# Transposing two MLP pieces at once, and placing the first piece's first product inside the attention's tail

## The chip, the cores and the metric

The kernel runs on one core of a Trainium2 chip. The metric is device time in microseconds for one execution. The kernel before took 525.93 us (median of 3 runs, 525.63 to 526.66). All durations below come from one profiled execution, which took 525.39 us and whose span, from its first to its last instruction, is 523.4 us.

## What is computed

The input x has 32 images of 32 by 32 positions with 64 channels, in float32. The reference is one block of a windowed transformer:

```
h = layernorm(x); roll by (-4,-4); cut into 8x8 windows
q,k,v = h @ qkv_w + qkv_b          # 4 heads of 16
attn = softmax(q k^T / 4 + relative position bias + mask)
x = x + roll_back(attn @ v @ proj_w + proj_b)
h2 = layernorm(x)
out = x + gelu(h2 @ fc1_w + fc1_b) @ fc2_w + fc2_b     # 64 -> 256 -> 64
```

## The kernel before

x stays in SBUF for the whole kernel, 128 partitions by 8 groups (GROUPS) of four images' rows. The attention runs first, as 64 steps (PAIRS) plus a tail of 4 (TAIL). Which tasks run at which step is a fixed list (TASKS, lines 81 to 98): XT transposes, QK and V products, Y the output projection. The last two Y tasks, (Y, last group, 0) and (Y, last group, 1), come at step 67.5, after everything else of the attention.

Then comes the MLP with its layer norm, in 32 pieces (S); a piece is 128 partitions by 512 numbers. Each engine has its own program and executes it in that order; semaphores are the only link. For a piece p the work is:

- DVE `sum2` (row sums, L406), GpSimd `centre2` (mean L323, then subtraction L338), ScalarE `square` (L590), DVE `square_sum` (L412), GpSimd `rstd` (add eps L330, then power -0.5, L333), DVE `scale_rows` (L420). That is the layer norm, and it leaves the piece in `xn`, which holds four pieces.
- TensorE `transpose_piece` (L829) into one of two PSUM banks, ScalarE `copy_xT2` (L672) into the buffer `xT2`.
- TensorE `fc1`, two halves of 4 instructions each (trans and outs, L693), ScalarE `gelu` per half (L678), TensorE `fc2` (work, 64 instructions, L693).
- DVE adds the result to x (L570, called out below) and has before that added the last bias to x (L581, called bf2 add below). SP stores.

The orders in the MLP, written out by hand, s counting from 0:

- TensorE (L887): transposes of s+1, fc1(s), fc2(s-1).
- ScalarE (L683): copy s+1, gelu(s) twice, square(s+3).
- DVE (L565): out(s-2), sum2(s+4), scale_rows(s+2), square_sum(s+3), bf2 add(s).
- GpSimd (L397): centre2(s+4) with its mean first, then rstd(s+3).

`centre2(s+4)` waits for the sum of that piece (L322) and for the transposes of piece s, whose place in `xn` it takes (L351). `scale_rows(u)` waits for rstd(u) (L417). `square(s+3)` stands behind both gelus of s on ScalarE. `fc1(s)` waits for the copy of s and for the gelus of s-1; `fc2(s)` for gelu(s) and for out(s-2). Transposes wait for the scaled piece.

Of the kernel before, what the change touches and what calls it, by code (L numbers as in the profile page):

```python
# [8 lines left out]
ACT = mybir.ActivationFunctionType  # L9
# [3 lines left out]
P = 128  # L13
BATCH, SIDE, C = 32, 32, 64
# [5 lines left out]
GROUPS = BATCH // GI  # L20
ROW = SIDE * C
PIECE = WIN * C
PIECES = ROW // PIECE
STEPS = 2 * GI
PAIRS = STEPS * GROUPS
BANK = 512
IMG = 4 * P
S = GROUPS * PIECES
# [37 lines left out]
TR, PV, OUT = 1, 2, 3  # L66
# [30 lines left out]
def tasks_at(n):  # L97
    return [task[1:] for task in TASKS if task[0] == n]
# [28 lines left out]
def build(nc, x_d, params_d, out_d):  # L127
    with ExitStack() as ctx:
        def sb(name, *shape, dtype=F32):
            return ctx.enter_context(nc.sbuf_tensor(name, [P, *shape], dtype))  # L130
# [57 lines left out]
        w1 = sb("w1", FF)  # L188
        bqkv = sb("bqkv", 2)
        bf1 = sb("bf1", 2)  # L190
        xT2 = [sb(f"xT2_{i}", BANK) for i in range(2)]
        hidden = [[probs[2 * i + half] for half in range(2)] for i in range(2)]


        xT2_bank = [scores[:, 0:BANK], scores[:, BANK:2 * BANK]]
        fc1_bank = [trans, outs2]
# [6 lines left out]
        w1_ready, biases_summed = sem("w1_ready"), sem("biases_summed")  # L203
        scores_ready, scores_taken = sem("scores_ready"), sem("scores_taken")
        negmax_ready, shifted, probs_ready = sem("negmax_ready"), sem("shifted"), sem("probs_ready")
        trans_ready, trans_copied = sem("trans_ready"), sem("trans_copied")
        outs_ready, inverse_ready, outs_taken = sem("outs_ready"), sem("inverse_ready"), sem("outs_taken")
        oT_ready, oT_copied = sem("oT_ready"), sem("oT_copied")
# [10 lines left out]
        xT2_ready, xT2_copied = sem("xT2_ready"), sem("xT2_copied")  # L219
        fc1_ready, gelu_done = sem("fc1_ready"), sem("gelu_done")  # L220
# [183 lines left out]
        def _(dve):  # L404
# [11 lines left out]
            def scale_rows(u, j):  # L416
                dve.wait_ge(ln_rstd, u + 1)  # L417
                chunk = xn[:, j * PIECE:(j + 1) * PIECE].rearrange("q (a f) -> q a f", f=C)
                r = stat_rstd[:, j * WIN:(j + 1) * WIN].unsqueeze(2).to_broadcast([P, WIN, C])
                nc.vector.tensor_tensor(chunk, chunk, r, ALU.mult).then_inc(xn_ready, 1)  # L420

            for t in range(2):
                done = nc.vector.memset(vX[t][:, :, :], 0.0)
# [4 lines left out]
            for column in ones:  # L428
                done = nc.vector.memset(column, 1.0)
# [6 lines left out]
            for half, i in ((second_half, 1), (first_half, 2), (second_half, 2), (first_half, 3),  # L436
                            (second_half, 3)):
                dst, src, c0, n = half(0, i)
# [124 lines left out]
            dve.wait_ge(y_added, COUNT["Y", GROUPS - 1, 1])  # L563

            for s in range(S + 2):  # L565
                if s >= 2:
                    dve.wait_ge(y2_ready, s - 1)
                    dve.wait_ge(bf2_added, s - 1)
                    dst = x[:, (s - 2) * PIECE:(s - 1) * PIECE]
                    nc.vector.tensor_tensor(dst, work[s % 2], dst, ALU.add).then_inc(out_ready, 1)  # L570
                if s + 4 < S:
                    sum2(s + 4)
                if PIECES <= s + 2 < S:
                    scale_rows(S + s + 2, (s + 2) % PIECES)
                if PIECES <= s + 3 < S:
                    square_sum(S + s + 3, (s + 3) % PIECES)
                if s < S:

                    dve.wait_ge(ln_centred, S + s + 1)
                    dst = x[:, s * PIECE:(s + 1) * PIECE].rearrange("q (a f) -> q a f", f=C)  # L580
                    nc.vector.tensor_tensor(dst, dst, bf2[:, :].unsqueeze(1).to_broadcast([P, WIN, C]),  # L581
                                            ALU.add).then_inc(bf2_added, 1)

        @block.scalar
        def _(act):
# [60 lines left out]
            def copy_oT(n):  # L646
# [6 lines left out]
                    outsT[:, 0:2 * P].rearrange("q (i a r) -> q i a r", i=2, r=WIN), ACT.Copy)\  # L653
                  .then_inc(oT_copied, 1)

            for n in range(PAIRS + TAIL):
                if n < PAIRS:
                    exp(n)
                squares_of(n)
                for kind, of, i in tasks_at(n):  # L660
                    take(kind, of, i)
                if 0 <= n - TR < PAIRS:
                    copy_trans(n - TR)
                if 0 <= n - OUT < PAIRS:
                    copy_oT(n - OUT)
                for kind, of, i in tasks_at(n + 0.5):
                    if kind != "Y":
                        take(kind, of, i)

            def copy_xT2(s):  # L670
                act.wait_ge(xT2_ready, s + 1)
                nc.scalar.activation(xT2[s % 2][:, :], xT2_bank[s % 2], ACT.Copy)\  # L672
                  .then_inc(xT2_copied, 1)

            def gelu(s):
                for half in range(2):
                    act.wait_ge(fc1_ready, 2 * s + half + 1)
                    nc.scalar.activation(hidden[s % 2][half][:, :], fc1_bank[half][:, :],  # L678
                                         ACT.Gelu_apprx_tanh, bias=bf1[:, half:half + 1])\
                      .then_inc(gelu_done, 1)  # L680

            copy_xT2(0)
            for s in range(S):  # L683
                if s + 1 < S:
                    copy_xT2(s + 1)
                gelu(s)
                if PIECES <= s + 3 < S:
                    square(S + s + 3, (s + 3) % PIECES, S + s + 4)

        @block.tensor  # L690
        def _(pe):
            def mm(out, lhsT, rhs, start=True, stop=True):
                return nc.tensor.matmul(out, lhsT, rhs, start=start, stop=stop)  # L693
# [127 lines left out]
            def transpose_piece(s):  # L821
                pe.wait_ge(xn_ready, S + s + 1)
                if s >= 2:
                    pe.wait_ge(xT2_copied, s - 1)
                else:
                    pe.wait_ge(scores_taken, PAIRS)
                for k in range(4):
                    at = s % PIECES * PIECE + k * P
                    done = nc.tensor.transpose(xT2_bank[s % 2][:, k * P:(k + 1) * P],  # L829
                                               xn[:, at:at + P], ident[:, :])  # L830
                done.then_inc(xT2_ready, 1)

            for kind, of, i in tasks_at(-1):
                if kind == "XT":
                    warm(2)
                fill(kind, of, i)
                if (kind, i) == ("QK", 0):
                    score(0)
            for n in range(PAIRS + TAIL):
                if n + 1 < PAIRS:  # L840
                    score(n + 1)
                for kind, of, i in tasks_at(n):
                    fill(kind, of, i)
                if 0 <= n - PV < PAIRS:
                    weigh(n - PV)
                if 0 <= n - TR < PAIRS:
                    transpose_probs(n - TR)
                if 0 <= n - OUT < PAIRS:
                    transpose_o(n - OUT)
                for kind, of, i in tasks_at(n + 0.5):  # L850
                    fill(kind, of, i)
                if n in (PAIRS, PAIRS + 1):
                    transpose_piece(n - PAIRS)

            pe.wait_ge(w1_ready, 1)
            pe.wait_ge(trans_copied, PAIRS)
            pe.wait_ge(oT_copied, PAIRS)
            copied("Y", GROUPS - 1, 1)

            def fc1(s):  # L860
                pe.wait_ge(xT2_copied, s + 1)
                for half in range(2):
                    if s:
                        pe.wait_ge(gelu_done, 2 * s - 1 + half)
                    for w in range(2):
                        rows = slice(C * w, C * (w + 1))
                        done = mm(fc1_bank[half][:, w * BANK:(w + 1) * BANK],
                                  w1[rows, half * P:(half + 1) * P], xT2[s % 2][rows, :])
                    done.then_inc(fc1_ready, 1)

            def fc2(s):

                if s >= 2:
                    pe.wait_ge(out_ready, s - 1)
                pe.wait_ge(gelu_done, 2 * s + 2)
                for k in range(4):
                    for w in range(2):
                        to = (2 * k + w) * C
                        for half in range(2):
                            for part in range(2):  # L880
                                at = w * BANK + k * P + part * C
                                done = mm(work[s % 2][C * part:C * (part + 1), to:to + C],
                                          hidden[s % 2][half][:, at:at + C], w2[:, half, :],
                                          start=half == 0, stop=half == 1)
                done.then_inc(y2_ready, 1)

            for s in range(S + 1):  # L887
                if 2 <= s + 1 < S:
                    transpose_piece(s + 1)
                if s < S:  # L890
                    fc1(s)
                if s:
                    fc2(s - 1)


def pack_params(ln1_g, ln1_b, qkv_w, qkv_b, proj_w, proj_b, rpb, ln2_g, ln2_b, fc1_w, fc1_b, fc2_w,
# [37 lines left out]
```

## Time and profile before

| | |
|---|---|
| median of 3 runs | 525.93 us |
| the profiled execution | 525.39 us |
| its span | 523.4 us |
| attention with its tail | 0 to 371 us |
| MLP, first fc1 to last add | 371 to 518 us |
| last stores | to 523.4 us |
| TensorE (PE) busy | 464.8 us |
| DVE / ScalarE / GpSimd busy | 391.3 / 361.6 / 384.0 us |
| granted TensorE clock, mean | 0.984 |

Busy is the time in which an engine had an instruction under way. PEld is TensorE's loading of weights, which overlaps its products. A row of the timeline has the start, the busy time, the engine, the line, what it writes and reads, and in square brackets how long the engine had been idle before it and what ended this.

### The profile page before, as it was taken

To read this page: it belongs to the slowest core of one execution; us is meant where nothing else is said; L and a number is where in the kernel's file an instruction comes from. 1 tells how busy PE (TensorE), PEld (TensorE's weight loads), DVE (VectorE), ACT (ScalarE), POOL (GpSimd) and SP (SyncE) were. 2 spreads that over 40 slices of the span, in tenths; PEclk is the share of its full clock that TensorE was granted. 3 is DMA by queue.
4 is the path that set the end of the run, shared out by engine and by line. 5 is a ranking of instruction groups with operands and counts; after the bars stand their busy time and mean duration, and the time that the engine had idled before them with its cause. 6 is when DMAs were issued, how large, how long until landed. Compare 5 with 4: busy or idle time off the path is not lost.

```text
span 523.4 us, 21507 instructions
## 1 busy us (share of the span) xinstructions
PE 464.8 (89%) x9630; PEld 351.7 (67%) x9630; DVE 391.3 (75%) x549; ACT 361.6 (69%) x501; POOL 384.0 (73%) x376
## 2 busy tenths in 40 slices
PE   0766798999999899899899899998799999999995
PEld 0534676777787787777778678687466666666664
DVE  2766797988889888888888888894367766666752
ACT  0245679768877867868878868775477777777762
POOL 2658889869868869869868968941278888888830
PEclk9997999999999999999999999999799999999998
DMA  8201441411501500511111011000003203311333
GB/s 160 58 1 41 105 94 42 113 24 28 118 23 25 123 23 24 117 29 24 27 30 33 23 29 38 23 23 3 1 3 84 66 19 81 83 39 46 82 83 81
DMA packets 9986, 27.04 MB, mean 52 GB/s; under 512 B 3368, under 2 KB 3368, under 8 KB 7976
## 3 DMA queue, kind: packets, MB, share of 16 engines
q1 hardware_dynamic: 9896, 25.68, 21.0%
q8 instruction: 76, 1.25, 1.0%
q14 instruction: 14, 0.11, 0.1%
HBM read 9.15 MB, written 8.39 MB: 34 GB/s over the span
## 4 chain that ended last, share of the span: by engine, by line
PE 61%; POOL 11%; DVE 11%; ACT 11%; issue 3%; DMA 2%; SPq 0%; ACTq 0%; DVEq 0%
PE work L693 20%; PE outs L693 13%; PE trans L693 8%; PE trans L789 7%; POOL probs L367 6%; PE scores L693 5%; PE scores L829 4%; ACT vX L612 3%; PE work L708 3%; ACT probsT L643 3%; DVE negmax L482 3%; POOL stat_rstd L333 3%; DVE probs L476 2%; DMA params<-in_params 2%; POOL xn L344 2%
## 5 line engine op out<-in xcount | busy, mean ns | idle before, releaser
L367 POOL TENSOR_TENSOR probs<-probs,negmax 128x1024 f32<-128x1024 f32 x64 | 121.7, 1902 | 36.0 <-DVE negmax L482 36.0
L333 POOL TENSOR_TENSOR stat_rstd<-stat_var,minus_half 128x8 f32<-128x8 f32 (+1 forms) x62 | 104.9, 1692 | 5.0
L476 DVE TENSOR_TENSOR probs<-scores,bias 128x1024 f32<-128x1024 f32 x64 | 77.9, 1218 | 28.4 <-PE scores L693 28.4
L638 ACT ACTIVATE probs<-probs 128x1024 f32<-128x1024 f32 x64 | 67.7, 1058 | 33.1 <-POOL probs L367 32.6
L643 ACT ACTIVATE probsT<-trans 128x1024 f32<-128x1024 f32 x64 | 65.6, 1024 | 31.8 <-PE trans L789 31.4
L693 PEld LDWEIGHTS outs<-vX,probsT 128*64 128x64 f32 x2048 | 65.0, 138 | 31.8 <-issue 29.4
L338 POOL TENSOR_TENSOR xn<-x,stat_mean 128x256 f32<-128x256 f32 (+1 forms) x91 | 77.2, 866 | 4.1
L482 DVE TENSOR_REDUCE negmax<-probs 128x16 f32<-128x1024 f32 x64 | 78.1, 1220 | 2.2
L693 PEld LDWEIGHTS work<-params,probs 128*64 128x64 f32 x2048 | 62.2, 138 | 23.5 <-DVE x L570 20.5
L693 PE MATMUL scores<-kX,qT 32*64 32x128 f32 x2048 | 71.5, 276 | 7.2 <-DVE probs L476 4.6
L693 PE MATMUL outs<-vX,probsT 128*64 128x34 f32 x2048 | 72.1, 225 | 2.2 <-ACT probsT L643 1.4
L789 PE MATMUL trans<-ident,probs 128*128 128x128 f32 x512 | 70.8, 282 | 0.0
L693 PE MATMUL work<-params,probs 128*64 128x64 f32 x2048 | 66.5, 223 | 0.0
L693 PEld LDWEIGHTS scores<-kX,qT 32*64 32x64 f32 x2048 | 55.9, 133 | 15.1 <-DMA kX<-kT 6.6
L412 DVE TENSOR_REDUCE stat_sq<-squares 128x8 f32<-128x512 f32 x64 | 43.0, 680 | 29.5 <-ACT squares L590 29.4
L789 PEld LDWEIGHTS trans<-ident,probs 128*128 128x128 f32 x512 | 55.5, 142 | 4.3 <-issue 1.6
L678 ACT ACTIVATE probs<-trans,bf 128x1024 f32<-128x1024 f32 x32 | 35.7, 1115 | 21.9 <-PE trans L693 21.9
L323 POOL TENSOR_TENSOR stat_mean<-stat_sum,one_over_c 128x8 f32<-128x8 f32 (+2 forms) x54 | 18.0, 334 | 43.6 <-DVE stat_sum L406 42.3
L590 ACT ACTIVATE squares<-xn 128x512 f32<-128x512 f32 x64 | 39.1, 621 | 15.3 <-DVE xn L439 15.3
L406 DVE TENSOR_REDUCE stat_sum<-x 128x8 f32<-128x512 f32 x64 | 42.2, 677 | 8.4 <-DMA x<-in_x 8.3
L330 POOL TENSOR_TENSOR stat_var<-stat_sq,eps 128x8 f32<-128x8 f32 (+1 forms) x62 | 23.3, 375 | 31.9 <-DVE stat_sq L412 31.9
L693 PE MATMUL work<-xT,wqkv 64*64 64x512 f32 x256 | 36.6, 629 | 7.8 <-DVE x L533 2.7
(64 smaller groups left out, 698.8 us busy)
## 6 DMA issues: line engine op xcount, KB each, us to landing
kX<-kT SPq DMA_DIRECT2D x124, 64.0 KB, 2.0
x<-in_x SPq DMA_DIRECT2D x32, 224.0 KB
out<-x SPq DMA_DIRECT2D x28, 224.0 KB
x<-in_x SPq DMA_DIRECT2D x32, 32.0 KB
out<-x SPq DMA_DIRECT2D x28, 32.0 KB
out<-x SPq DMA_DIRECT2D x16, 56.0 KB
params<-in_params SPq DMA_DIRECT2D x1, 741.5 KB, 11.8
out<-x SPq DMA_DIRECT2D x16, 8.0 KB
```

Source lines behind the costliest of these rows:

```text
L333: nc.gpsimd.tensor_tensor(stat_rstd[:, cols], stat_var[:, cols], minus_half[:, cols], ALU.pow).then_inc(ln_rstd, pieces)
L338: return nc.gpsimd.tensor_tensor(dst, src.rearrange("q (a f) -> q a f", f=C), m, ALU.add)
L367: nc.gpsimd.tensor_tensor(e, e, top, ALU.add).then_inc(shifted, 1)
L406: nc.vector.tensor_reduce(stat_sum[:, r * WIN:(r + 1) * WIN], src.rearrange("q (a f) -> q a f", f=C), AXX, ALU.add, negate=True).then_inc( ...
L412: nc.vector.tensor_reduce(stat_sq[:, r * WIN:(r + 1) * WIN], squares[r % PIECES][:, :].rearrange("q (a f) -> q a f", f=C), AXX, ALU.add).t ...
L476: nc.vector.tensor_tensor(e[:, :].rearrange("q (u a m) -> q a u m", u=2, a=2), scores[:, :].rearrange("q (a u m) -> q a u m", a=2, u=2), b ...
L482: nc.vector.tensor_reduce(negmax[n % 4][:, :], e[:, :].rearrange("q (a m) -> q a m", m=N), AXX, ALU.max, negate=True).then_inc(negmax_read ...
L590: nc.scalar.activation(squares[j % PIECES][:, :], xn[:, j * PIECE:(j + 1) * PIECE], ACT.Square, scale=float(C) ** -0.5).then_inc(ln_square ...
L638: nc.scalar.activation(probs[n % 4][:, :], probs[n % 4][:, :], ACT.Exp)\
L643: nc.scalar.activation(probsT[n % 2][:, :], trans[:, :], ACT.Copy)\
L693: return nc.tensor.matmul(out, lhsT, rhs, start=start, stop=stop)
L789: done = nc.tensor.transpose(trans[:, t * P:(t + 1) * P], probs[n % 4][:, t * P:(t + 1) * P], ident[:, :])
```

## The change

The transposes of the pieces s+1 and s+2 now stand together, for odd s, between fc1(s) and fc2(s-1); before, those of s+1 stood ahead of fc1(s). `xT2` has four buffers and not two. ScalarE copies both pieces behind gelu(s) for odd s; square(s+3) follows the copies. On DVE, scale_rows(s+2) moves from behind out(s-2) and sum2(s+4) to ahead of both. fc1(0) leaves the MLP: its first half is put in step 66 of the attention's loop, its second half between the two last Y tasks; ScalarE copies pieces 0 and 1 inside that loop too. GpSimd's program is not touched.

```diff
-        xT2 = [sb(f"xT2_{i}", BANK) for i in range(2)]
+        xT2 = [sb(f"xT2_{i}", BANK) for i in range(4)]
...
             for s in range(S + 2):
+                if PIECES <= s + 2 < S:
+                    scale_rows(S + s + 2, (s + 2) % PIECES)
                 if s >= 2:
                     dve.wait_ge(y2_ready, s - 1)
                     dve.wait_ge(bf2_added, s - 1)
@@
                 if s + 4 < S:
                     sum2(s + 4)
-                if PIECES <= s + 2 < S:
-                    scale_rows(S + s + 2, (s + 2) % PIECES)
                 if PIECES <= s + 3 < S:
                     square_sum(S + s + 3, (s + 3) % PIECES)
...
+                if n in (PAIRS, PAIRS + 1):
+                    copy_xT2(n - PAIRS)
...
-            copy_xT2(0)
             for s in range(S):
-                if s + 1 < S:
-                    copy_xT2(s + 1)
                 gelu(s)
+                if s % 2:
+
+                    for t in (s + 1, s + 2):
+                        if t < S:
+                            copy_xT2(t)
                 if PIECES <= s + 3 < S:
                     square(S + s + 3, (s + 3) % PIECES, S + s + 4)
...
                 for kind, of, i in tasks_at(n + 0.5):
                     fill(kind, of, i)
+                    if (kind, of, i) == ("Y", GROUPS - 1, 0):
+                        fc1(0, 1)
                 if n in (PAIRS, PAIRS + 1):
                     transpose_piece(n - PAIRS)
-
-            pe.wait_ge(w1_ready, 1)
-            pe.wait_ge(trans_copied, PAIRS)
-            pe.wait_ge(oT_copied, PAIRS)
+                if n == PAIRS + OUT - 1:
+
+                    pe.wait_ge(w1_ready, 1)
+                    pe.wait_ge(trans_copied, PAIRS)
+                    fc1(0, 0)
+
             copied("Y", GROUPS - 1, 1)
...
-            for s in range(S + 1):
-                if 2 <= s + 1 < S:
-                    transpose_piece(s + 1)
+            for s in range(1, S + 1):
                 if s < S:
-                    fc1(s)
-                if s:
-                    fc2(s - 1)
+                    for half in range(2):
+                        fc1(s, half)
+                if s % 2:
+                    for t in (s + 1, s + 2):
+                        if t < S:
+                            transpose_piece(t)
+                fc2(s - 1)
```

## Rows read from the trace of the kernel before

**Rows 1.** Busy time by engine, a stretch of the MLP: PE, PEld, DVE, ACT, POOL.
```profile
420.00:440.00 20.00, 20.00 (x350) 13.90 (x346) 13.88 (x23) 14.06 (x19) 16.44 (x18) 1.00 0.23 56
```
**Rows 2.** Chain that ended last, same stage: start, us, work.
```profile
387.47 2.02 PE work L693 x64
```
**Rows 3.** Timeline of one piece in the MLP's steady state, all engines.
```profile
385.42 0.68 DVE L581 TENSOR_TENSOR x<-x,params 128x512 f32<-128x512 f32 x1
...
385.48 1.13 PE L693 MATMUL trans<-xT,w 64*128 64x512 f32 x4
385.58 0.58 POOL L330 TENSOR_TENSOR stat_var<-stat_sq,eps 128x8 f32<-128x8 f32 x1 [0.58 <-DVE stat_sq L412]
...
386.01 0.68 DVE L570 TENSOR_TENSOR x<-work,x 128x512 f32<-128x512 f32 x1
...
386.24 1.65 POOL L333 TENSOR_TENSOR stat_rstd<-stat_var,minus_half 128x8 f32<-128x8 f32 x1
386.45 1.02 PE L693 MATMUL outs<-xT,w 64*128 64x512 f32 x4
...
386.62 0.68 DVE L406 TENSOR_REDUCE stat_sum<-x 128x8 f32<-128x512 f32 x1
...
387.40 2.08 PE L693 MATMUL work<-params,probs 128*64 128x64 f32 x64
...
387.85 0.20 POOL L323 TENSOR_TENSOR stat_mean<-stat_sum,one_over_c 128x8 f32<-128x8 f32 x1
387.92 0.69 DVE L420 TENSOR_TENSOR xn<-xn,stat_rstd 128x512 f32<-128x512 f32 x1 [0.63 <-POOL stat_rstd L333]
388.13 1.38 POOL L338 TENSOR_TENSOR xn<-x,stat_mean 128x512 f32<-128x512 f32 x1
388.67 0.63 ACT L590 ACTIVATE squares<-xn 128x512 f32<-128x512 f32 x1
389.33 0.69 DVE L412 TENSOR_REDUCE stat_sq<-squares 128x8 f32<-128x512 f32 x1 [0.72 <-ACT squares L590]
...
389.42 0.66 PE L829 MATMUL scores<-ident,xn 128*128 128x128 f32 x4
...
390.00 1.13 PE L693 MATMUL trans<-xT,w 64*128 64x512 f32 x4
390.10 0.58 POOL L330 TENSOR_TENSOR stat_var<-stat_sq,eps 128x8 f32<-128x8 f32 x1 [0.58 <-DVE stat_sq L412]
```
**Rows 4.** Timeline of TensorE in an attention step: eight transposes.
```profile
349.16 1.09 PE L789 MATMUL trans<-ident,probs 128*128 128x128 f32 x8
```
**Rows 5.** Instructions of single lines: ns min/median/max; the third is GpSimd's subtraction.
```profile
L517 DVE TENSOR_TENSOR x<-x,y_bias x16: 1215/1783/2966, 54.4 to 348.4; 128x1024 f32<-128x1024 f32 x16
...
L330 POOL TENSOR_TENSOR stat_var<-stat_sq,eps x62: 200/208/585, 19.4 to 503.1; 128x8 f32<-128x8 f32 x60, 128x16 f32<-128x16 f32 x2
...
L338 POOL TENSOR_TENSOR xn<-x,stat_mean x28: 1042/1378/1380, 372.3 to 496.6; 128x512 f32<-128x512 f32 x28
```
**Rows 6.** Timeline of the attention's tail and the MLP's first product.
```profile
365.49 1.08 ACT L672 ACTIVATE xT<-scores 128x512 f32<-128x512 f32 x2
365.74 1.16 PE L693 MATMUL work<-params,oT 64*64 64x64 f32 x64 [0.56 <-ACT oT L651]
...
368.23 1.16 PE L693 MATMUL work<-params,oT 64*64 64x64 f32 x64 [1.34 <-DVE x L527]
...
371.07 2.08 PE L693 MATMUL trans<-xT,w 64*128 64x512 f32 x4 [1.68 <-DVE x L533]
```
**Rows 7.** Busy time by engine and granted clock (last but two) around that product.
```profile
366.80:370.27 3.47, 1.26 (x71) 1.02 (x64) 2.03 (x3) 1.07 (x1) 0.00 (x0) 1.00 0.02 5
370.27:377.10 6.83, 6.03 (x16) 2.75 (x18) 2.43 (x5) 2.76 (x3) 2.83 (x4) 0.50 0.00 0
```
**Rows 8.** Timeline of the MLP's end: last first product, last add.
```profile
511.46 1.13 PE L693 MATMUL trans<-xT,w 64*128 64x512 f32 x4
...
517.37 0.69 DVE L570 TENSOR_TENSOR x<-work,x 128x512 f32<-128x512 f32 x1 [1.18 <-PE work L693]
```

More of the change, by code:

```diff
@@ L654, in copy_oT, with copy_xT2 @@
                   .then_inc(oT_copied, 1)
+            def copy_xT2(s):
+                act.wait_ge(xT2_ready, s + 1)
+                nc.scalar.activation(xT2[s % 4][:, :], xT2_bank[s % 2], ACT.Copy)\
+                  .then_inc(xT2_copied, 1)
             for n in range(PAIRS + TAIL):
@@ L668, in _ @@
                         take(kind, of, i)
[L670 to L673, printed above, removed]
+                if n in (PAIRS, PAIRS + 1):
+                    copy_xT2(n - PAIRS)
             def gelu(s):
@@ L831, in transpose_piece, with fc1 @@
                 done.then_inc(xT2_ready, 1)
+            def fc1(s, half):
+                pe.wait_ge(xT2_copied, s + 1)
+                if s:
+                    pe.wait_ge(gelu_done, 2 * s - 1 + half)
+                for w in range(2):
+                    rows = slice(C * w, C * (w + 1))
+                    done = mm(fc1_bank[half][:, w * BANK:(w + 1) * BANK],
+                              w1[rows, half * P:(half + 1) * P], xT2[s % 4][rows, :])
+                done.then_inc(fc1_ready, 1)
             for kind, of, i in tasks_at(-1):
@@ L851, in _ @@
                     fill(kind, of, i)
+                    if (kind, of, i) == ("Y", GROUPS - 1, 0):
+                        fc1(0, 1)
                 if n in (PAIRS, PAIRS + 1):
                     transpose_piece(n - PAIRS)
-            pe.wait_ge(w1_ready, 1)
-            pe.wait_ge(trans_copied, PAIRS)
-            pe.wait_ge(oT_copied, PAIRS)
+                if n == PAIRS + OUT - 1:
+                    pe.wait_ge(w1_ready, 1)
+                    pe.wait_ge(trans_copied, PAIRS)
+                    fc1(0, 0)
             copied("Y", GROUPS - 1, 1)
-            def fc1(s):
-                pe.wait_ge(xT2_copied, s + 1)
-                for half in range(2):
-                    if s:
[L864 to L869, printed above, removed]
             def fc2(s):
@@ L885, in fc2 @@
                 done.then_inc(y2_ready, 1)
-            for s in range(S + 1):
-                if 2 <= s + 1 < S:
-                    transpose_piece(s + 1)
+            for s in range(1, S + 1):
                 if s < S:
-                    fc1(s)
-                if s:
-                    fc2(s - 1)
+                    for half in range(2):
[5 more added lines that the diff above has]
+                fc2(s - 1)
 def pack_params(ln1_g, ln1_b, qkv_w, qkv_b, proj_w, proj_b, rpb, ln2_g, ln2_b, fc1_w, fc1_b, fc2_w,
```

## The prediction

> **What bounds the kernel now.** I read the busy time by stretch first, to see which engine is full in the stage that changes, then the chain of waits, then the timeline of one piece. In the MLP's steady state TensorE is busy for all of 20.00 us, GpSimd for 16.44, ScalarE and DVE for about 14 [rows 1]. The chain there is TensorE alone; its costliest link is the second product with 2.02 us [rows 2]. The timeline gives the steps of TensorE, start to start: first half of fc1 0.97 (385.48 to 386.45), second half 0.95 (to 387.40), fc2 2.02 (to 389.42), four transposes 0.58 (to 390.00). The sum is 4.52 us a piece [rows 3]. Nothing of this is a wait. The layer norm runs beside it with little to spare: GpSimd waited 0.58 us for the sums of squares and DVE 0.63 us for rstd, once a piece [rows 3]. So the question is not only what TensorE saves, but whether the norm's ring through DVE and GpSimd still closes within a piece's time. It has to be followed in the order of the programs.
>
> **What TensorE saves.** Eight transposes took 1.09 us [rows 4] and four took 0.66 [rows 3], so four more in the same run cost 0.43 and not 0.58. A pair of pieces would take 0.97+0.95+0.58+0.43+2.02+0.97+0.95+2.02 = 8.89 us against 9.04. The switches from fc1 to transposes and from transposes to fc2 are not in the trace; the nearest are fc1 to fc2 (in the 0.95) and transposes to fc1 (in the 0.58). I give them 0.1 either way, so 15 pairs save 2.3 us, between -0.7 and 5.3, if nothing waits.
>
> fc1(0) leaves the path. Its first half now stands where TensorE was idle for 0.56 us [rows 6] and takes 0.97, so the first of the two last projections starts 0.4 later at most; I take 0.4. Its second half (0.95) lies in the 1.34 us in which TensorE waits for DVE between them [rows 6], and costs nothing; were that idle time not there, it would cost its 0.95. The copies of pieces 0 and 1 on ScalarE (1.08 for both) started at 365.49 [rows 6] and now stand ahead of the last copy of the attention's output by one copy; it is inside the same 0.4. fc1(1) can then start at 371.07 + 0.4 = 371.47, where fc1(0) started. Two more buffers of xT2 cost no time.
>
> **What the move on DVE does.** This decides. GpSimd's order stays centre2(s+4), rstd(s+3). Before, DVE issued sum2(s+4) ahead of scale_rows(s+2), so that GpSimd got its sum while DVE waited for rstd. Now DVE waits for rstd(s+2) first, and out(s-2), sum2(s+4), square_sum(s+3) and the bf2 add are queued behind that wait. rstd(s+3) on GpSimd stands behind centre2(s+4), which needs sum2(s+4). This closes a ring with one piece in it: scale(k), out, sum2(k+2), mean, centre2(k+2), rstd(k+1), scale(k+1). A faster TensorE does not shorten it. Its length, call the start of scale(k) zero:
>
> - scale to out 0.61 and out to sum2 0.61 (one DVE step each, 386.01 to 386.62) [rows 3];
> - sum2 to mean 0.77 (as 389.33 to 390.10, DVE's reduction to GpSimd's next), mean to subtraction 0.28 (387.85 to 388.13) [rows 3]: the subtraction starts at 2.27 and takes 1.04, its shortest time [rows 5], to 3.31;
> - DVE reaches the bf2 add at 0.61 x 4 = 2.44, while GpSimd subtracts. An addition of two SBUF operands on DVE does not run beside a GpSimd one: that of L517 took between 1215 and 2966 ns for the same work [rows 5], and the subtraction took 1378 instead of 1042 where a scale_rows had started just ahead of it [rows 3, 5]. So I let the add wait until 3.31. From the start of such an add to the start of the power is 0.82 (385.42 to 386.24), which is 4.13;
> - power to scale_rows 1.68 (386.24 to 387.92) [rows 3]. The ring takes 5.81 us.
>
> Without the add in the way the step from add-eps to power would be 0.28 (as mean to subtraction; add-eps itself takes 200 ns at least) and the ring 0.61+0.61+0.77+0.28+1.04+0.28+1.68 = 5.27. If the mean too were held up (585 instead of 200 ns) and the subtraction took 1.38, it would be 6.53 [rows 5]. I take 5.81, for which each meeting has its row.
>
> The Trainium skill (SBUF — State Buffer, SBUF: two separate sides) says that GpSimd and a DVE instruction with two SBUF inputs take a shared pair of ports as an exclusive lock, for a whole instruction. The trace agrees with its 1215 to 2966 ns. By that rule the ring is 5.81, without it 5.27, which is 14 us over the kernel.
>
> TensorE needs 8.89/2 = 4.45 a piece, so it waits for the ring. Is anything slower than the ring? The squares of an odd piece t stand behind both gelus of t-3 and meet an earlier deadline than before: from fc1(t-3) to square(t) 3.19 (385.48 to 388.67), to its sum 0.66, to add-eps 0.77, to the power 0.66 (385.58 to 386.24), to scale_rows 1.68, and 0.77 to its transposes (0.69 and an estimated hand-over of 0.08): 7.73 us [rows 3]. fc1(t-3) starts 0.58 + 2.02 after the transposes of t-2; together 10.33 us a pair, less than the ring's 2 x 5.81 = 11.62. So the ring ends last, and TensorE stands idle once a pair for 11.62 - 8.89 = 2.7 us, between the transposes of an even and of an odd piece.
>
> **The sum.** fc1(1) at 371.47. square(4) follows it by 3.19 and the two copies, 1.08 [rows 6], at 375.74; its sum 0.66, add-eps 0.77, power 0.66 and 1.68 later scale(4) starts, at 379.51. The ring goes round for each k from 4 to 29: 26 x 5.81 = 151.1, scale(30) at 530.6. Piece 31 has no subtraction before it: 0.61+0.61+0.77+0.66+1.68 = 4.33, scale(31) at 534.9, its transposes at 535.7. Then, with nothing in the way, transposes 0.58, fc2 2.02, fc1 1.92, fc2 2.02, and from the last fc1 to the last add 5.91 (511.46 to 517.37) [rows 8]: 548.1. From the last add to the end of the span were 6.03 us, the span to the time 1.99, and the profiled execution lies 0.54 below the median: 556.7 us. To this I add 2 for the clock (below): 558.5 us, 33 slower than 525.93.
>
> **The clock.** In the MLP's first 6.83 us TensorE had 1.2 GHz granted, after a stretch of 3.47 us in which it was busy for 1.26 [rows 7]; four instructions took 2.08 us there against 1.13 [rows 3, 6]. With fc1(0)'s second half in that stretch it is busy for 2.2, and the fall may stay out. But the new gaps of 2.7 us are of the same kind. A fall costs little while the ring has slack: the squares' path above, held against the ring, has 1.3 us a pair. Over 6.83 us at that ratio 6.83 - 6.83 x 1.13/2.08 = 3.1 us of work are lost, so up to 1.8 in such a pair. I count one such fall in the forecast.
>
> **The rivals.**
>
> A. TensorE's order alone decides (faster). It needs the ring under 4.45 us, that is that DVE's sums run ahead of the scaling after all. For it: the 0.58 and 0.63 of slack [rows 3], and TensorE the bound everywhere. Against it: the two waits stand in the programs. From fc1(1) at 371.47, 15 x 8.89 to fc1(31) at 504.8, 5.9 to the last add at 510.7 instead of 517.4: 519.3 us.
>
> B. The ring is looser than I read it, and only the squares' path holds: 14 odd pieces (5 to 31) at 10.33 - 8.89 = 1.44 each on A's time, 539.5 us. For it: the steps of GpSimd could be shorter when it does not wait. Against it: the ring would have to be under 5.2, below its shortest rows.
>
> C. TensorE's clock falls in every gap. The squares' path then ends last in each pair: 13 x 1.8 on 556.7 is 580 us. For it: the row of 1.26 in 3.47 us [rows 7]. Against it: TensorE works for 8.9 us without a break between gaps. The Trainium skill (TensorE: Matmul & The Clock Gate, HAM oscillation — how this bites in real kernels) tells of a kernel that lost its clock in every wait for a transfer. That speaks against this change; here the trace shows one fall in front of the MLP and none inside it, where TensorE never waited.
>
> **How the numbers follow.** Forecast 0.80, A 0.05, B 0.06, C 0.07; 0.02 is left for a result within 0.2% of before, which is about what a measurement can tell from no change (gain and loss in balance by accident). The range: the short ring (5.27) gives 542.7 + 2 for the clock, about 545; upward a ring of 6.2 gives 567, with two or three falls of the clock 571. B and C lie outside. Faster is A, 0.05; slower 0.93.
>
> **What would show it.** In the profile after: the scale_rows instructions about 5.8 us apart all through, with DVE waiting some 1.8 us ahead of each for the power, and GpSimd waiting ahead of each mean for the row sum, about 2 us (before: not at all); TensorE idle once a pair for 2.7 us ahead of the transposes, released by DVE; the chain led by GpSimd and DVE instead of TensorE. The saving on TensorE is right if a pair without the gap is 8.9 us. fc1(0)'s halves should stand ahead of and between the last two projections, and fc1(1) start near 371.5. The prediction is wrong if sum2 is seen to start before the power of two pieces earlier has ended, or if the distance between scalings is under 5.2 us.

## The result, and the profile after

The changed kernel took 557.27 us (median of 4 runs, 555.46 to 558.25) against 525.78 us before on the same chip: 1.0594 times as long, 95% interval 1.0559 to 1.0629. Forecast were 558.5 us, within 545 to 571. The profiled execution took 558.25 us with a span of 556.2 us, 32.8 more than before.

The chain that ended last, from the page of the changed kernel, led by TensorE with 61% before, now runs over four engines. Over the whole kernel TensorE still has the largest share; between 385 and 535 us, where the loss arises, GpSimd leads it with 22.0% for the power, 9.7% for the subtraction and 8.0% for add-eps, against 12.9% for TensorE's fc2.

```profile
PE 38%; POOL 25%; ACT 13%; DVE 12%; issue 9%; DMA 2%; SPq 0%; POOLq 0%; ACTq 0%; DVEq 0%
```

The stretch that [rows 1] shows before, in the same columns. TensorE was busy for all of it; now it is for 16.55 us of 20, at a mean granted clock of 0.91, and no other engine is full either. So no engine's amount of work sets the pace here. The next two views show what does.

```profile
420.00:440.00 20.00, 16.55 (x258) 11.44 (x260) 12.05 (x18) 10.78 (x15) 11.46 (x13) 0.91 0.22 54
```

The view of who waited for whom, between 390 and 530 us (total us, times, longest). Each of DVE and GpSimd now waits for the other once a piece, 24 times each, by amounts that do not vary (48.0 us in 24 waits is 2.0 each, which is also the longest); TensorE waits for the scaling once a pair.

```profile
POOL stat_mean L323 <- DVE stat_sum L406: 48.0, 24, 2.0
...
DVE xn L420 <- POOL stat_rstd L333: 43.8, 24, 1.8
...
PE scores L833 <- DVE xn L420: 21.7, 12, 2.3
```

One turn of the ring and the start of the next, from the timeline of the changed kernel, to be held against [rows 3]. It is read down: addition, row sum, mean, subtraction, add-eps, power, scaling, addition.

```profile
427.34 0.68 DVE L572 TENSOR_TENSOR x<-work,x 128x512 f32<-128x512 f32 x1
...
427.94 0.68 DVE L406 TENSOR_REDUCE stat_sum<-x 128x8 f32<-128x512 f32 x1
...
428.70 0.20 POOL L323 TENSOR_TENSOR stat_mean<-stat_sum,one_over_c 128x8 f32<-128x8 f32 x1 [2.00 <-DVE stat_sum L406]
...
428.98 1.04 POOL L338 TENSOR_TENSOR xn<-x,stat_mean 128x512 f32<-128x512 f32 x1
429.13 1.44 DVE L581 TENSOR_TENSOR x<-x,params 128x512 f32<-128x512 f32 x1
...
429.98 0.66 POOL L330 TENSOR_TENSOR stat_var<-stat_sq,eps 128x8 f32<-128x8 f32 x1
430.23 0.42 PEld L833 LDWEIGHTS scores<-ident,xn 128*128 128x128 f32 x4 [0.76 <-issue]
430.24 0.65 PE L833 MATMUL scores<-ident,xn 128*128 128x128 f32 x4
...
430.71 1.65 POOL L333 TENSOR_TENSOR stat_rstd<-stat_var,minus_half 128x8 f32<-128x8 f32 x1
...
432.39 0.69 DVE L420 TENSOR_TENSOR xn<-xn,stat_rstd 128x512 f32<-128x512 f32 x1 [1.83 <-POOL stat_rstd L333]
433.00 0.68 DVE L572 TENSOR_TENSOR x<-work,x 128x512 f32<-128x512 f32 x1
...
433.14 0.66 PE L833 MATMUL scores<-ident,xn 128*128 128x128 f32 x4 [2.25 <-DVE xn L420]
```

From addition to addition 5.66 us (427.34 to 433.00). The bf2 add took 1.44 us instead of 0.68: it waited for the subtraction to end at 430.02, and add-eps behind it took 0.66 instead of 0.20. TensorE's even piece was transposed at 430.24, the odd one had to wait until 433.14.

The next turn took 5.70 us (scaling to scaling, 432.39 to 438.09), and its last wait is another. Here add-eps starts 0.76 us behind the start of the sum of squares, the usual hand-over. That sum had waited for its square, and the square stood on ScalarE behind the copy of the odd piece:

```profile
433.83 0.60 ACT L658 ACTIVATE xT<-scores 128x512 f32<-128x512 f32 x1 [1.73 <-PE scores L833]
434.32 0.62 ACT L590 ACTIVATE squares<-xn 128x512 f32<-128x512 f32 x1
...
434.98 0.69 DVE L412 TENSOR_REDUCE stat_sq<-squares 128x8 f32<-128x512 f32 x1 [0.70 <-ACT squares L590]
...
435.74 0.58 POOL L330 TENSOR_TENSOR stat_var<-stat_sq,eps 128x8 f32<-128x8 f32 x1
```

So a second ring of nearly the same length lies beside the first: scaling, transposes, copy, square, sum of squares, add-eps, power, scaling. Turns of 5.66 and of 5.69 to 5.73 alternate, but for those behind a fall of TensorE's clock (below).

**Where the 32.8 us of the span are.** scale(4) started at 380.36 (before 383.40): -3.0. From there to scale(30) 150.1 us passed against 117.5: +32.6. From scale(30) to scale(31) 6.16 against 4.51: +1.6. From scale(31) to the last add 13.19 against 11.94: +1.2. The last stores: +0.4.

### The profile page after: what moved, and what is told of

Its sections match the earlier page's. It is cut to its first block, busy times and chain, and to the rows that moved or that the text cites. A ratio compares the mean times of both kernels' runs of the same rounds, so it can differ in the third digit from the quotient of the medians.

```text
span 556.2 us, 21537 instructions
## 1 busy us (share of the span) xinstructions
PE 471.5 (85%) x9630; PEld 358.1 (64%) x9630; DVE 394.3 (71%) x549; ACT 359.9 (65%) x501; POOL 376.7 (68%) x376
## 4 chain that ended last, share of the span: by engine, by line
PE 38%; POOL 25%; ACT 13%; DVE 12%; issue 9%; DMA 2%; SPq 0%; POOLq 0%; ACTq 0%; DVEq 0%
PE work L697 12%; POOL stat_rstd L333 10%; PE outs L697 8%; PE trans L793 7%; POOL probs L367 7%; PE scores L697 3%; ACT vX L612 3%; PE work L712 3%; ACT probsT L643 3%; POOL xn L338 3%; POOL stat_var L330 3%; PE trans L697 3%; ACT probs L680 2%; POOL xn L344 2%; DVE stat_sq L412 2%
## 5 line engine op out<-in xcount | busy, mean ns | idle before, releaser
L697 PEld LDWEIGHTS work<-params,probs 128*64 128x64 f32 x2048 | 69.3, 150 | 14.8 <-issue 12.6
L697 PE MATMUL work<-params,probs 128*64 128x64 f32 x2048 | 73.7, 236 | 0.0
L338 POOL TENSOR_TENSOR xn<-x,stat_mean 128x256 f32<-128x256 f32 (+1 forms) x91 | 68.5, 772 | 4.1
L420 DVE TENSOR_TENSOR xn<-xn,stat_rstd 128x512 f32<-128x512 f32 x32 | 22.0, 691 | 52.6 <-POOL stat_rstd L333 52.6
```

What stands on the lines that cost most here:

```text
L338: return nc.gpsimd.tensor_tensor(dst, src.rearrange("q (a f) -> q a f", f=C), m, ALU.add)
```

## The experiments

In all of them the ratio is to the kernel before, run beside it on the same chip; the experiments ran on three chips, so kernels are best compared by ratio. The single runs of the kernel before lay between 522.14 and 528.66 us over the three sets.

**The move on DVE alone.**

```
             for s in range(S + 2):
+                if PIECES <= s + 2 < S:
+                    scale_rows(S + s + 2, (s + 2) % PIECES)
                 if s >= 2:
...
-                if PIECES <= s + 2 < S:
-                    scale_rows(S + s + 2, (s + 2) % PIECES)
```

> The kernel before with one edit: on DVE scale_rows(s+2) stands ahead of out(s-2) and sum2(s+4), as in the change. TensorE, ScalarE and the attention's tail are as before. Ring theory (scaling, out, row sum, mean, subtraction, rstd, next scaling, one piece in it): the ring closes with TensorE's old order too, scalings 5.7 us apart, TensorE idle 1.2 us once a piece, about 555 us. Rival (the pairs of transposes are what costs, the move on DVE is harmless): scalings stay 4.52 apart and the time stays at 526 +-1 us.

554.25 us, ratio 1.0573 (1.0537 to 1.0609). This is what the ring theory gave (about 555). Two moved lines make nearly the whole loss. The timeline of this kernel shows the ring with TensorE's old order, 5.65 us from scaling to scaling, and TensorE idle once a piece:

```profile
431.08 0.69 DVE L420 TENSOR_TENSOR xn<-xn,stat_rstd 128x512 f32<-128x512 f32 x1 [1.82 <-POOL stat_rstd L333]
...
431.83 0.66 PE L829 MATMUL scores<-ident,xn 128*128 128x128 f32 x4 [1.06 <-DVE xn L420]
...
436.73 0.69 DVE L420 TENSOR_TENSOR xn<-xn,stat_rstd 128x512 f32<-128x512 f32 x1 [1.82 <-POOL stat_rstd L333]
```

**The change without the move.** The same edit the other way round, in the changed kernel.

> The changed kernel with scale_rows(s+2) put back behind sum2(s+4); pairs of transposes and the early fc1(0) stay. Ring theory: the ring is open; what is left is the path from fc1(s) for even s over the square behind its gelus to the transposes of s+3, 10.3 to 10.6 us a pair of pieces against 8.9 of TensorE's work: 539 to 544 us. Rival 1 (the pairs alone make the whole loss): 557 us as the change. Rival 2 (the pairs are harmless once the ring is open): 519 us.

538.46 us, ratio 1.0276 (1.0247 to 1.0305). Both rivals fall, and the time is just under the 539 to 544 expected. The scalings come 4.61 and 5.69 us apart in turn, 10.30 a pair (forecast 10.33 for this path). The losses of e1 and of this kernel do not add up to that of the change (5.7% and 2.8% against 5.9%): each piece waits only for the path that ends last. In the timeline the odd piece's square starts at 432.36, behind both gelus; the odd piece is scaled at 436.13 and TensorE waits 1.20 us for it:

```profile
432.36 0.63 ACT L590 ACTIVATE squares<-xn 128x512 f32<-128x512 f32 x1
433.03 0.69 DVE L412 TENSOR_REDUCE stat_sq<-squares 128x8 f32<-128x512 f32 x1 [0.81 <-ACT squares L590]
...
436.13 0.69 DVE L420 TENSOR_TENSOR xn<-xn,stat_rstd 128x512 f32<-128x512 f32 x1 [0.62 <-POOL stat_rstd L333]
...
436.88 0.66 PE L833 MATMUL scores<-ident,xn 128*128 128x128 f32 x4 [1.20 <-DVE xn L420]
```

**Squares earlier.** On top of the last kernel:

```
             for s in range(S):
+                if PIECES <= s + 3 < S:
+                    square(S + s + 3, (s + 3) % PIECES, S + s + 4)
                 gelu(s)
...
-                if PIECES <= s + 3 < S:
-                    square(S + s + 3, (s + 3) % PIECES, S + s + 4)
```

> The kernel of e2 (pairs, scaling back in its old place) with square(s+3) on ScalarE ahead of both gelus of s and not behind them and the copies. If the path of e2 is what it is taken for, the square comes 2 us earlier (ScalarE is idle then) and the pair falls to 9.0 to 9.5 us: 521 to 529 us. Rival (e2's loss is a wait of TensorE on something else, the copies or the gelus): as e2, 539 to 544 us, or more, since the gelus now come 0.6 us later.

520.0 us, ratio 0.9920 (0.9891 to 0.9949): 0.8% less than before, small but clear of 1, and below the stated span of 521 to 529. The pair now takes 8.90 us, all of it TensorE's work. Once more with more rounds:

> e4's kernel again, beside e9 on one chip, with more rounds, to settle which of the two is the faster one. In its profile a pair of pieces took 8.90 us (before 9.04), but its second and third pair 9.19 and 9.59. 15 x 0.14 = 2.1 us less than e9, minus some 0.6 for the first pairs: 519.5 to 520.5 us, 1 to 2 us under e9. Rival (the pair saves nothing that can be told): as e9.

520.63 us, ratio 0.9922 (0.9892 to 0.9953), 0.1 above the expected span. The steps of a pair in its timeline, start to start: fc1 0.96 and 0.96, eight transposes 1.03, fc2 2.02; then fc1 0.96 (440.65 to 441.61).

```profile
435.68 1.13 PE L697 MATMUL trans<-xT,w 64*128 64x512 f32 x4
...
436.64 1.02 PE L697 MATMUL outs<-xT,w 64*128 64x512 f32 x4
...
437.60 1.10 PE L833 MATMUL scores<-ident,xn 128*128 128x128 f32 x8
...
438.63 2.08 PE L697 MATMUL work<-params,probs 128*64 128x64 f32 x64
...
440.65 1.13 PE L697 MATMUL trans<-xT,w 64*128 64x512 f32 x4
```

(The expectation's 9.19 and 9.59 were sums of two distances of scalings in the first profile; only the start of the stage has them.)

**Squares earlier, but with the move.** Is it the squares alone, then?

> The changed kernel with square(s+3) ahead of the gelus, and scale_rows left where the change puts it. Ring theory: the squares are not in the ring, so it still turns once in 5.7 us, and only the few turns are shorter that waited for a square: 553 to 556 us. Rival (late squares are the whole cause, as e4 might be read): 520 us as e4.

551.75 us, ratio 1.0500 (1.0454 to 1.0547). The rival falls: every one of 26 turns took 5.65 to 5.67 us. The squares are not in the first ring, and moving them does not shorten it. The 5.70 of every second turn is gone, and with it the second ring. The time is below the 553 to 556 expected. The clock fell four times in this kernel's MLP without lengthening a turn, since the earlier squares give that path slack.

**The early fc1(0) alone.** The changed kernel with the MLP's three programs put back as before:

```
+            transpose_piece(2)
             for s in range(1, S + 1):
+                if s >= 2 and s + 1 < S:
+                    transpose_piece(s + 1)
                 if s < S:
                     for half in range(2):
                         fc1(s, half)
-                if s % 2:
-                    for t in (s + 1, s + 2):
-                        if t < S:
-                            transpose_piece(t)
                 fc2(s - 1)
```

> The kernel before with the early fc1(0) alone (halves in the attention's tail, pieces 0 and 1 copied there); all orders of the MLP as before. Theory: fc1(0) leaves the path and TensorE's clock does not fall at the MLP's start; fc1(1) starts 3.8 us earlier than before (375.83 to 372.0), the rest keeps 4.52 us a piece: 522.0 +-0.5 us. Rival (the projections and the final adds are pushed back by as much as is saved, or the clock falls later instead): 525 to 526 us.

521.06 us, ratio 0.9941 (0.9918 to 0.9963), somewhat better than the 522.0 +-0.5 expected. Once more, beside the kernel of e8:

> e3's kernel again, beside e8: 521 us +-0.7, with one piece in 4.52 us all through and no fall of the clock at the MLP's start.

521.98 us, ratio 0.9949 (0.9925 to 0.9973), 0.3 above the expected span. On the two chips it was 1.1 and 1.35 us behind the pairs with early squares. The intervals of the ratios overlap, but six of e8's eight runs are below the fastest of e9's twelve, and the profiles show 8.90 against 9.04 us a pair.

**The pairs with early squares, without the early fc1(0).**

> e4's kernel with fc1(0) back in its old place behind the last projection. It tells what the early fc1(0) is worth by itself. In the profiles the stretch from the attention's last weighing to fc1(1) was 13.13 us before, 10.87 in e1 (no fall of the clock there) and 9.19 with transposes of one piece in e3: the early place saves 1.7 us where the clock does not fall and 3.9 where it falls. So 521.5 to 524 us, 1.7 to 3.9 over e8. Rival (TensorE's first product was never on the path): as e8.

523.69 us, ratio 0.9955 (0.9923 to 0.9986). The twelve runs are of two kinds, five from 520.14 to 521.13 and seven from 523.27 to 525.46. The profiled one took 524.11 and has TensorE's clock at 1.2 GHz for 6.8 us from 371.3 on; fc1(0) starts at 372.13. If that fall is what parts the two groups, the early place is worth mostly the fall that it avoids. This is not shown: one execution of the slower group was profiled and none of the faster, and the mean granted clocks (0.990 to 0.991 in the faster, 0.986 to 0.991 in the slower) overlap. The faster group is level with e8, where 1.7 us had been expected; why stays open.

**Without the bf2 add.** This kernel leaves out the second product's bias; the result's addition waits for the subtraction in its place.

```
-                    dve.wait_ge(bf2_added, s - 1)
+                    dve.wait_ge(ln_centred, S + s - 1)
...
-                if s < S:
-
-                    dve.wait_ge(ln_centred, S + s + 1)
-                    dst = x[:, s * PIECE:(s + 1) * PIECE].rearrange("q (a f) -> q a f", f=C)
-                    nc.vector.tensor_tensor(dst, dst, bf2[:, :].unsqueeze(1).to_broadcast([P, WIN, C]),
-                                            ALU.add).then_inc(bf2_added, 1)
```

> The changed kernel without the bf2 add (the bias of the second product is left out of the computation; out(s-2) waits for the subtraction in its place). It tests the term of 0.82 in the ring: the add waits for GpSimd's subtraction and then holds up add-eps. If they exclude each other, the add's 1.44 us go back to 0 and the ring falls from 5.68 to 5.3 us; 26 turns make 10 us: 546 to 548 us. Rival (the two engines do not hinder each other, the long durations are only how a queue is recorded): ring 5.68 and 556 to 557 us.

543.3 us, ratio 1.0372 (1.0337 to 1.0408). The turns fell to 5.21 and 5.32 us in turn (forecast 5.27 for a ring without this meeting); the longer ones are those of the second ring, through the copy and the square. The time is below the 546 to 548 expected: the clock did not fall in this kernel's MLP, so the long turns are gone as well. Its timeline has add-eps at 0.20 and the power 0.28 behind it:

```profile
433.35 0.68 DVE L406 TENSOR_REDUCE stat_sum<-x 128x8 f32<-128x512 f32 x1
...
434.11 0.20 POOL L323 TENSOR_TENSOR stat_mean<-stat_sum,one_over_c 128x8 f32<-128x8 f32 x1 [2.00 <-DVE stat_sum L406]
...
434.39 1.04 POOL L338 TENSOR_TENSOR xn<-x,stat_mean 128x512 f32<-128x512 f32 x1
...
435.39 0.20 POOL L330 TENSOR_TENSOR stat_var<-stat_sq,eps 128x8 f32<-128x8 f32 x1
435.67 1.65 POOL L333 TENSOR_TENSOR stat_rstd<-stat_var,minus_half 128x8 f32<-128x8 f32 x1
```

**Work in TensorE's gap.** Two products on unused data, ahead of the wait for an odd piece.

```
             def transpose_piece(s):
-                pe.wait_ge(xn_ready, S + s + 1)
                 if s >= 2:
                     pe.wait_ge(xT2_copied, s - 1)
...
+                if s >= 5 and s % 2:
+                    for _ in range(2):
+                        mm(xT2_bank[s % 2], ident[:, :], params[:, 0:BANK])
+                pe.wait_ge(xn_ready, S + s + 1)
```

> The changed kernel with two products of 128x512 on unused data in TensorE's gap ahead of each odd piece's transposes, into the bank that the transposes then overwrite; nothing else is touched. Clock term: TensorE's clock fell in 6 of the change's gaps, and the turn of the ring behind each fall took 6.14 instead of 5.68 us. If the falls cost that, the time goes down by 6 x 0.45 = 2.7 us, to 554.5, and all turns take 5.68. Rival (the long turns come from something else, the stores for example): as the change, 557 +-1. If the dummies reach past the gap the time goes up.

553.99 us, ratio 1.0582 (1.0536 to 1.0628): by the time alone this cannot be told from the change's 1.0594. The time is as forecast (554.5), and the profiles can tell. The first row is this kernel's, the second the changed kernel's, for the same stretch (granted clock last but two):

```profile
385.00:535.00 150.00, 142.54 (x2077) 89.67 (x2078) 91.74 (x132) 83.31 (x105) 89.85 (x103) 1.00 0.19 46
```
```profile
385.00:535.00 150.00, 126.49 (x1972) 87.10 (x1972) 86.48 (x129) 80.46 (x103) 88.77 (x103) 0.93 0.18 44
```

The clock stayed at 2.4 GHz throughout and no turn took over 5.70 us. In the changed kernel it fell six times, for 3.4 us each, and one turn behind each fall took 6.1 to 6.2. How a fall gets into the ring, in the changed kernel's timeline and windows: fc2 took 2.95 us instead of 2.08, the first half of fc1 1.83 instead of 1.13, together 1.6 us of work lost, and the square behind it kept DVE waiting for 1.19 us. The squares' path has 11.36 - 10.30 = 1.06 us of slack in a pair, so some 0.5 of the 1.6 is left over.

```profile
434.65:438.07 3.42, 3.42 (x44) 2.68 (x42) 1.28 (x2) 0.29 (x1) 3.26 (x3) 0.50 0.00 0
```
```profile
433.72 2.95 PE L697 MATMUL work<-params,probs 128*64 128x64 f32 x64
...
436.60 1.83 PE L697 MATMUL trans<-xT,w 64*128 64x512 f32 x4
...
441.16 0.69 DVE L412 TENSOR_REDUCE stat_sq<-squares 128x8 f32<-128x512 f32 x1 [1.19 <-ACT squares L590]
```

**GpSimd's order turned too.** In the changed kernel:

```
             for s in range(S - 2):
-                if s + 4 < S:
-                    centre2(s + 4)
                 if s + 3 >= PIECES and s + 3 < S:
                     rstd(S + s + 3, (s + 3) % PIECES)
+                if s + 4 < S:
+                    centre2(s + 4)
```

> The changed kernel with GpSimd's order turned as well: rstd(s+3) ahead of centre2(s+4), so that the ring no longer has the row sum and the subtraction in it. By the order of the programs alone the ring is scaling, out, row sum, sum of squares, add-eps, power: 3 x 0.61 + 0.77 + 0.28 to 0.82 + 1.68 = 4.6 to 5.1 us, 531 to 543 us. Rival, DVE's scaling and GpSimd's subtraction exclude each other: the subtraction starts just behind the power, the scaling waits for its end, about 0.9 more, and with the bf2 add as well 5.8 to 5.9 us a piece: 556 to 560 us, no gain at all.

554.85 us, ratio 1.0591 (1.0554 to 1.0628). The expected 531 to 543 is missed. No gain, as the rival had it (556 to 560), but for neither of its reasons. The scaling was not held up; it came first and the subtraction waited (1.38 us). The turns took 5.39 or 5.69 us, and 6.15 to 6.17 behind a fall of the clock. The timeline shows another ring in place of the first: power, mean, subtraction, square, sum of squares, add-eps, power, since the piece subtracted behind one power is the one that the next needs. From power to power 5.39 (400.80 to 406.19); the turns of 5.69 are again those in which the square stands behind the copy of the odd piece.

```profile
400.80 1.65 POOL L333 TENSOR_TENSOR stat_rstd<-stat_var,minus_half 128x8 f32<-128x8 f32 x1
...
402.42 0.20 POOL L323 TENSOR_TENSOR stat_mean<-stat_sum,one_over_c 128x8 f32<-128x8 f32 x1
402.48 0.69 DVE L420 TENSOR_TENSOR xn<-xn,stat_rstd 128x512 f32<-128x512 f32 x1 [1.82 <-POOL stat_rstd L333]
402.70 1.38 POOL L338 TENSOR_TENSOR xn<-x,stat_mean 128x512 f32<-128x512 f32 x1
...
404.11 0.63 ACT L590 ACTIVATE squares<-xn 128x512 f32<-128x512 f32 x1 [0.68 <-POOL xn L338]
...
404.77 0.69 DVE L412 TENSOR_REDUCE stat_sq<-squares 128x8 f32<-128x512 f32 x1 [0.40 <-ACT squares L590]
...
405.54 0.58 POOL L330 TENSOR_TENSOR stat_var<-stat_sq,eps 128x8 f32<-128x8 f32 x1 [1.46 <-DVE stat_sq L412]
...
406.19 1.65 POOL L333 TENSOR_TENSOR stat_rstd<-stat_var,minus_half 128x8 f32<-128x8 f32 x1
```

## Why the prediction was right, step by step

- **The ring.** Right in kind, place and number of turns; e1 shows that it needs only the move on DVE, e2 that it is gone without. Forecast 5.81, measured 5.66 and 5.70, 5.68 in the mean. The term that was too long is from the end of the subtraction to the power: 0.69 instead of 0.82, since the bf2 add, having waited, ended 0.55 us behind the subtraction (430.57 against 430.02) and not 0.68. Over 26 turns that is 3.4 us too much. The forecast had the add meet the subtraction in every turn. In every second one it came only at 435.58, when the subtraction was all but over, and the second ring set the turn; that its length came out within 0.04 us of the first is luck.
- **The two SBUF operands.** e5 shows the meeting: the first ring took 5.21 without the add, where 5.27 had been worked out, and the subtraction's end to the power 0.24 (435.43 to 435.67) instead of 0.69. The exclusive lock that the Trainium skill states (SBUF — State Buffer, SBUF: two separate sides) agrees with the add's 1.44 us, and in e7 with the subtraction's 1.38 behind a scaling.
- **The squares' path.** 10.33 a pair forecast, 10.30 measured once the ring was open (e2). Rival B's time, 539.5, was what the change would have cost without the move: 538.46.
- **The pair's saving.** 8.89 us a pair forecast, 8.90 measured where nothing waits (e8). In the whole kernel it made 1.1 to 1.35 us (e4 against e3, e8 against e9) of the 2.3 counted. Rival A, 519.3 us, is about what the change gives once both paths are out of the way: 520.63.
- **The early fc1(0).** The first of the last two projections started 1.40 us behind the last transposes of the attention's output (365.88 to 367.28), where it had been 0.98 before: 0.4 later, as taken. No fall of the clock was seen there in the changed kernel. fc1(1) started at 372.42 instead of 371.47; the attention itself had ended 1.1 us later in this execution (last weighing at 363.82 instead of 362.70).
- **The clock.** Undersized as a whole, by two errors that offset each other: too few falls, each too dear. One was counted, at up to 1.8 us, from a fall of 6.83 us. (The sum says 2, but 556.7 and 2 are 558.7; the 558.5 holds the 1.8.) There were six, of 3.4 us: five turns longer by 0.45 us, and the last step, scale(30) to scale(31), 6.16 instead of the 4.33 of the sum (e6 4.6, e1 4.3 without a fall): some 3.8 us.
- **The end.** From the transposes of the last piece (537.33) to the last add (549.78) 12.45 us, as summed.

The nearness of 558.5 to 557.27 owes something to luck, since terms cancel. The ring was 3.4 us too long; the clock was 2.0 too short and the last step another 0.3, fc1(1) came 0.95 later and the stores took 0.4 more. Then the profiled execution lies 0.98 above the median of its kernel, where the sum took it to lie 0.54 below, 1.5 the other way. Rival C was the right mechanism at a fraction of its price: the falls came in six of 14 gaps, and the squares' slack took most of each.

## What to carry to other kernels

Before an instruction is moved ahead of another in an engine's program, write down what it waits for and follow that chain through the other engines' programs until it comes back: if what it overtakes feeds its own next turn, the move closes a ring whose length is the sum of latencies, and no engine will look full. Then look for the second ring behind the first, because opening one (e2, e7) shows the next; here the pairs of transposes paid only when the ring and the late squares were both out of the way, and then little. With the pairs, the early squares and the early fc1(0) the ratio was 0.9922 (e8), with the early fc1(0) alone 0.9949 (e9), with the pairs and the early squares alone 0.9955 (e10). What marked the ring in this case was a profile with every engine at 54 to 83% and two engines that waited for each other by a constant length.

## What was not expected of the hardware

In the changed kernel's MLP TensorE had 14 gaps, one a pair: one of 2.88 us, seven of 2.25 and six of 1.20, the latter in the pairs slowed by a fall. The granted clock fell to 1.2 GHz for 3.4 us behind the gap of 2.88 and behind five of the seven of 2.25, each time 0.1 to 1.5 us after TensorE had resumed work, and behind none of 1.20. So a fall shortens the next gap, and behind a short gap none was seen. The other kernels agree: four falls with eight gaps of 2.2 (e11), one behind a gap of 2.60 and four with eight of 1.98 (e7), none with gaps of 1.06 (e1), of 1.20 (e2) and of 1.41 (e5, whose first gap was 2.04). Why some gaps of 2.25 had a fall and two had none stays open.

The start of the MLP can come out in two ways as well. The profiled execution of the kernel before had a fall there. e1's, with the same instructions up to there, had not: from the first fc1 to the first fc2 7.29 us (371.07 to 378.36) against 4.42 (370.73 to 375.15). Whether e10's two groups, whose medians lie 3.9 us apart, are this is not shown.
